# Feed-forward stage of a graph layer: TensorE's output projection ahead of the third chunk of the first layer, and the second layer's first two columns in three chunks

## The chip, the cores and the metric

One Trainium2 chip, one core. The metric is the device time of one execution in microseconds (us), as the median of several runs. An engine executes its own instructions in order; engines wait for each other through semaphores (`wait_ge` on the one side, `then_inc` on the other).

## The reference, cut to what matters

Two graph layers over 12500 nodes of 128 features and 200000 edges. The first is attention over edges and then a feed-forward part; the part that the change touches is:

```python
        att = agg.reshape(n, NH * HD) @ Wo + bo
        x = residual + att
        residual = x
        h = _layer_norm(x, g2, b2)
        ffn = jax.nn.gelu(h @ W1 + bf1, approximate=False) @ W2 + bf2
        return residual + ffn
```

`agg` is the softmax-weighted sum over a node's edges and its own loop. HID is 128, FFN is 512. Around it stand an outer residual and, ahead of the second layer, `relu(layernorm(x))`; its rows go to a table (`h_tab` in the trace, `h2_tab` in the code) that the second layer gathers.

## The kernel before, in words

The kernel goes through its stages in turn: a preparation with queries, keys and values (group_a), the edges of the first layer (batch_b), the nodes of the first layer (group_c), the edges of the second layer (batch_d), the nodes of the second layer (group_e). Each stage has a loop on each engine, and the order of the work on an engine is written out by hand. The change lies in group_c, on TensorE (PE) and on ScalarE (ACT).

group_c goes over 14 groups of 896 nodes; a group is 128 partitions by G = 7 columns of 128 features. Buffers are doubled: group g uses set k = g mod 2. Group g's steps are:

- VectorE (DVE), `attend`: weighs and adds the gathered states, divides, and writes the aggregate `qg` (L1866, counts `agg_s`). It then copies the indices for GpSimd's next gathers (L1868).
- TensorE transposes the seven columns of `qg` (L1335, counts `aggT_ps`), ScalarE copies them (L1154, counts `aggT_s`), TensorE multiplies by `wo` (L1343, counts `att_ps`): this is the projection of attention.
- VectorE, `add_attention`: adds it to the nodes (L1875) and takes their statistics (L238, L243). ScalarE takes the square root (`norm_root`, L248). VectorE inverts it (L254, L256) and writes the normalised rows `hn2` (L1833, counts `hn2_s`).
- TensorE transposes `hn2` (`norm_T`, L1302); ScalarE copies with scale and bias (`norm2_T`, L1113).
- TensorE, `ffn1` (L1311): the first layer in FC = 4 chunks of 128 hidden features, each two matmuls of 448 columns. Chunks alternate between two pairs of PSUM banks, so chunk 2 waits for gelu 0 and chunk 3 for gelu 1. ScalarE, `gelu` (L1143, counts `gelu_s`), one for each chunk.
- TensorE, `ffn2` (L1322): the second layer, seven columns of four chunks each, accumulated in PSUM. It writes the banks that chunks 0 and 2 used. Ahead of column FFN_COLUMNS = 5 it places `norm_T` of the next group.
- VectorE, `add_ffn`: adds the result (L1886) and takes statistics; ScalarE, `norm3` (L1123), writes the normalised rows for the second graph layer, seven columns spread over the gaps between gelus of a later group. SyncE stores them; GpSimd adds the outer residual and the bias by DMA (L904, L910) and gathers the next states (L635).

A 32-bit matmul appears as two instructions in the trace: `ffn1` has 16 rows a group, `ffn2` 56, the projection 14. Transposes have 7.

The groups are interleaved. In turn g, TensorE's order before is: chunks 0 and 1 of group g-1, transposes of group g, chunk 2 of g-1, projection of g, chunk 3 of g-1, five columns of `ffn2` of g-1, `norm_T` of g, two columns of `ffn2` of g-1. ScalarE's order is: `norm2_T` and gelu 0 of g-1, two columns of `norm3`, the copy of the transposes of g, gelus 1 to 3 of g-1 with one column of `norm3` behind each, then the roots (a table load before them), the exponentials of the loops (another table load), an activation that loads the gelu table (a third), and two columns of `norm3`. VectorE's order is `add_attention` of g-1, the scale and `hn2` of g-1, the aggregate of g, `add_ffn` of g-2, and the maxima for g+1.

Of the kernel before, what the change touches and what calls it, by code (L numbers as in the profile page):

```python
# [31 lines left out]
FC = FFN // P  # L32
# [4 lines left out]
G = 7  # L37
# [36 lines left out]
FIRST_COLUMNS = 2  # L74
COLUMNS_BY = (4, 5, 6, G)
FFN_COLUMNS = 5
BANK_COLUMNS = ((0, 4), (4, G))
QKV_BANKS = 4
SHIFT_COLUMN = 3
# [47 lines left out]
def build(nc, a, out):  # L127
    ctx = ExitStack()
    with ctx:
# [79 lines left out]
        def two_banks(b):  # L209

            flat = ps[:, b:b + 2, :].rearrange("p a b -> p (a b)")
            return flat[:, 0:GW], [flat[:, j * HID:(j + 1) * HID] for j in range(G)]
# [7 lines left out]
        def halves(b):  # L220

            return ps[:, b:b + 2, 0:HALF]
# [23 lines left out]
        def norm_root(act, ln, n):  # L246
            act.wait_ge(ln.steps, n * 4 - 2)
            nc.scalar.activation(ln.dev, ln.mean_var[:, :, 1], ACT.Sqrt, bias=eps_t[:]).then_inc(ln.std, 1)  # L248
# [256 lines left out]
        def last_group(g):  # L505
            return isinstance(g, int) and g == 2 * PAIRS - 1
# [461 lines left out]
        def _(act):  # L968
# [141 lines left out]
            def norm2_T(g, k):  # L1110

                act.wait_ge(hnT2_ps, g + 1)
                nc.scalar.activation(xT[k], two_banks(4 * k)[0], ACT.Identity, bias=cols[:, 3:4], scale=cols[:, 2:3])\  # L1113
                    .then_inc(hnT2_s, 1)

            def norm3(g, k, start, stop, stored=None):

                if stored is not None:
                    act.wait_ge(h2_stored[k], stored)
                act.wait_ge(lnC[1].steps, g * 4 + 4)  # L1120
                settle(act)
                for j in range(start, stop):
                    done = nc.scalar.activation(h2b[k][:, j, :], column(nodes, g * G + j), ACT.Relu,  # L1123
                                                bias=nmr3[k][:, j:j + 1], scale=rstd3[k][:, j:j + 1])
                if stop == G:
                    done.then_inc(h2_s, 1)

            def gelus(g, k, norm3_too, start=0, stop=FC):


                for c in range(start, stop):
                    j = COLUMNS_BY[c - 1] if c else FIRST_COLUMNS
                    act.wait_ge(ff1_ps, g * FC + c + 1)
                    gelu(g, k, c)
                    if norm3_too and j < COLUMNS_BY[c]:
                        norm3(g - 2, k, j, COLUMNS_BY[c])

            def loop_exp(g, k):
                act.wait_ge(low1_s, g + 1)
                nc.scalar.activation(w_c[k], low_c[k], ACT.Exp, scale=SCALE).then_inc(w_cs, 1)  # L1140

            def gelu(g, k, c):
                nc.scalar.activation(gT[k][:, c, :].rearrange("p (h f) -> p h f", h=2),  # L1143
                                     halves(4 * k + 2 - 2 * (c % 2)), ACT.Gelu, bias=bf1[:, c:c + 1]).then_inc(gelu_s, 1)

            def group_c(i, first):

                for k in range(2):
                    g = i * 2 + k
                    if not (first and k == 0):  # L1150
                        norm2_T(g - 1, 1 - k)
                        gelus(g - 1, 1 - k, not (isinstance(g, int) and g < 3), 0, 1)
                    act.wait_ge(aggT_ps, g + 1)
                    nc.scalar.copy(xT[k], two_banks(4 * k)[0]).then_inc(aggT_s, 1)  # L1154
                    if not (first and k == 0):
                        gelus(g - 1, 1 - k, not (isinstance(g, int) and g < 3), 1, FC)

                    norm_root(act, lnC[0], g + 1)
                    if not first:
                        norm_root(act, lnC[1], g - 1)  # L1160
                    if not last_group(g):
                        loop_exp(g + 1, 1 - k)
                    nc.scalar.activation(gelu_load, eps_t[:], ACT.Gelu)
                    if not first:
                        norm3(g - 2, k, 0, FIRST_COLUMNS, None if isinstance(i, int) and i == 1 else i * 16 - 16)
            loop_exp(0, 0)
            repeat(act, PAIRS, group_c, peel=2, tail=1)
            norm2_T(2 * PAIRS - 1, 1)
            gelus(2 * PAIRS - 1, 1, True)
# [56 lines left out]
        def _(pe):  # L1226
# [54 lines left out]
            for t in range(2):  # L1281
                done = nc.tensor.matmul(ps[:, t, :], ones[:], diag8[:, 4 * t:4 * t + 4, :].rearrange("p h c -> p (h c)"),  # L1282
                                        start=True, stop=True)
            done.then_inc(chunk_ps, 1)
            pe.wait_ge(chunk_s, 5)
            for h in range(NH):
                done = nc.tensor.transpose(ps[:, 2 + h // 4, (h % 4) * P:(h % 4 + 1) * P], weight[:, h, :], ident[:])
# [3 lines left out]
            for h in range(NH):  # L1291
                nc.tensor.matmul(ps[:, 4, h * HD:(h + 1) * HD], weightT[:, h, :],
                                 stb[LAST][:, B - 1, h * HD:(h + 1) * HD], start=True, stop=True)
                done = nc.tensor.matmul(ps[:, 4, HID + h:HID + h + 1], weightT[:, h, :],
                                        stb[LAST][:, B - 1, HID + h:HID + h + 1], start=True, stop=True)
# [3 lines left out]
            def norm_T(g, k):  # L1299
                pe.wait_ge(hn2_s, g + 1)  # L1300
                for j in range(G):
                    done = nc.tensor.transpose(two_banks(4 * k)[1][j], hn2[:, j, :], ident[:])  # L1302
                done.then_inc(hnT2_ps, 1)

            def ffn1(g, k, chunks):
                pe.wait_ge(hnT2_s, g + 1)
                for c in chunks:
                    if c >= 2:
                        pe.wait_ge(gelu_s, g * FC + c - 1)
                    for h in range(2):  # L1310
                        done = nc.tensor.matmul(halves(4 * k + 2 - 2 * (c % 2))[:, h, :], w1[:, c * P:(c + 1) * P],  # L1311
                                                xT[k][:, h * HALF:(h + 1) * HALF], start=True, stop=True)
                    done.then_inc(ff1_ps, 1)

            def ffn2(g, k, between):

                pe.wait_ge(gelu_s, g * FC + FC)
                for j in range(G):
                    if between and j == FFN_COLUMNS:
                        norm_T(g + 1, 1 - k)  # L1320
                    for c in range(FC):
                        done = nc.tensor.matmul(two_banks(4 * k + 2)[1][j], gT[k][:, c, j * HID:(j + 1) * HID], w2[:, c, :],  # L1322
                                                start=(c == 0), stop=(c == FC - 1))
                done.then_inc(ff2_ps, 1)

            def group_c(i, first):
                for k in range(2):
                    g = i * 2 + k
                    if first and k == 1:
                        norm_T(0, 0)  # L1330
                    if not (first and k == 0):
                        ffn1(g - 1, 1 - k, range(0, 2))
                    pe.wait_ge(agg_s, g + 1)
                    for j in range(G):
                        done = nc.tensor.transpose(two_banks(4 * k)[1][j], qg[k][:, j, :], ident[:])  # L1335
                    done.then_inc(aggT_ps, 1)
                    if not (first and k == 0):
                        ffn1(g - 1, 1 - k, range(2, 3))
                    pe.wait_ge(aggT_s, g + 1)
                    if not first:  # L1340
                        pe.wait_ge(x2_s, g - 1)
                    for j in range(G):
                        done = nc.tensor.matmul(two_banks(4 * k + 2)[1][j], xT[k][:, j * HID:(j + 1) * HID], wo[:],  # L1343
                                                start=True, stop=True)
                    done.then_inc(att_ps, 1)
                    if not (first and k == 0):
                        ffn1(g - 1, 1 - k, range(3, FC))
                        ffn2(g - 1, 1 - k, True)
            repeat(pe, PAIRS, group_c)
            ffn1(2 * PAIRS - 1, 1, range(FC))  # L1350
            ffn2(2 * PAIRS - 1, 1, False)


# [8 lines left out]
            def group_e(i, first):  # L1362
                for k in range(2):
# [12 lines left out]
                    done.then_inc(mlp1_ps, 1)  # L1376
                    for j0, j1 in BANK_COLUMNS:
                        nc.tensor.matmul(flat[:, j0 * HID:j1 * HID].rearrange("p (j f) -> p j f", f=HID), ones[0:1, :],
                                         gb2[0:1, :].unsqueeze(1).to_broadcast([1, j1 - j0, HID]), start=True, stop=False)
                    pe.wait_ge(relu_s, g + 1)  # L1380
                    for j0, j1 in BANK_COLUMNS:
                        for j in range(j0, j1):
# [622 lines left out]
```

## Time and profile before

| | us |
|---|---|
| median of 3 runs | 4827.98 |
| lowest to highest | 4821.74 to 4830.42 |
| the profiled execution | 4826.0 |
| its span in the trace | 4824.4 |

| engine | busy us | share |
|---|---|---|
| PE matmul | 507.4 | 11% |
| PE weight load | 356.6 | 7% |
| DVE | 2847.1 | 59% |
| ACT | 2136.2 | 44% |
| POOL | 3407.3 | 71% |

The shares are means over stages with different limits, so the rows further down are from the stage itself, which lies between about 2400 and 2675 us. A timeline row has its start, how long it lasts, engine, line, operation, the tile written and those read, and the number of instructions merged into it; in brackets stands how long the engine was idle before it and who released it. The end of a row of matmuls lies about 0.15 us past the start of the next, since they are pipelined.

### The profile page before, as it was taken

Reading aid. Unit: us, or ns where it says so; the run is one execution under the profiler, and the core shown is the slowest. Engines: PE = TensorE matmul, PEld = TensorE weight load, DVE = VectorE, ACT = ScalarE, POOL = GpSimd, SP = SyncE. Lnnn points to the kernel's source line nnn. Section 1 sums busy time; section 2 is a strip of 40 time slices with the busy share of each in tenths; the row PEclk is TensorE's granted clock in tenths of the full one; section 3 lists DMA queues with packets and bytes.
Section 4 is the critical chain, followed back from the end, with each engine's and each line's share of the span. In section 5 each row is a group of like instructions: output and inputs, shape, how many; then the busy total and the mean of one; then the engine's idle time right before and its main releaser. Section 6 shows DMA issues by size and latency. Waiting matters only on the chain.

```text
span 4824.4 us, 22224 instructions
## 1 busy us (share of the span) xinstructions
PE 507.4 (11%) x2377; PEld 356.6 (7%) x2377; DVE 2847.1 (59%) x4386; ACT 2136.2 (44%) x2140; POOL 3407.3 (71%) x3610
## 2 busy tenths in 40 slices
PE   4620000000000000000189000000000000000007
PEld 2410000000000000000067000000000000000004
DVE  7837999999999999999778222222222222222223
ACT  4414555454444555554367344444444444444432
POOL 4677777777777777777554677777777777777766
PEclk8655555555555555555599555555555555555558
DMA  9995666666666666666455233333333333333334
GB/s 360 381 370 182 218 211 212 214 214 216 214 213 214 214 214 216 211 211 210 151 119 125 93 102 101 101 105 102 104 104 104 104 104 104 104 104 104 104 98 138
DMA packets 235483, 816.46 MB, mean 169 GB/s; under 512 B 67005, under 2 KB 93789, under 8 KB 185242
## 3 DMA queue, kind: packets, MB, share of 16 engines
q1 hardware_dynamic: 77464, 457.58, 25.5%
q0 software_dynamic: 143232, 344.58, 25.0%
q10 hardware_dynamic: 14722, 13.70, 0.9%
q14 instruction: 57, 0.47, 0.0%
q8 instruction: 8, 0.13, 0.0%
HBM read 455.00 MB, written 354.21 MB: 168 GB/s over the span
## 4 chain that ended last, share of the span: by engine, by line
POOL 42%; issue 19%; DVE 15%; DMA 10%; DVEq 7%; PE 5%; ACT 1%; SPq 0%; POOLq 0%; ACTq 0%
POOL arena L635 41%; DMA q_edges<-arena 7%; DVE ps L1689 4%; DMA arena<-kv_tab,idx 2%; DVE ps L1735 2%; DVE arena L1682 2%; PE ps L1322 2%; PE ps L1311 2%; DVE arena L1751 2%; DVEq L1706 2%; DVEq L1776 2%; DVEq L1718 2%; DVE ps L1631 1%; DVEq L1723 1%; DVE ps L1713 1%
## 5 line engine op out<-in xcount | busy, mean ns | idle before, releaser
L635 POOL DMA_INDIRECT arena<-h_tab,idx x1568 | 1479.7, 944 | 520.4 <-issue 500.1
L635 POOL DMA_INDIRECT arena<-kv_tab,idx x1568 | 1482.6, 946 | 506.9 <-issue 493.5
L1927 DVE SCALAR_TENSOR_TENSOR ps<-arena,keep,ps 128x128 f32<-128x128 f32 x97 | 42.4, 438 | 1486.4 <-ACT ps L1193 1486.4
L1193 ACT COPY ps<-arena 128x2048 f32<-128x2048 f32 x97 | 347.9, 3587 | 768.1 <-DMA arena<-h_tab,idx 768.1
L1206 ACT COPY arena<-arena 128x2048 f32<-128x2048 f32 x97 | 354.2, 3652 | 402.2 <-DVE arena L1934 402.2
L1631 DVE TENSOR_TENSOR_SCAN ps<-arena,ps 128x256 f32<-128x256 f32 (+2 forms) x584 | 502.4, 860 | 0.3
L1058 ACT COPY arena<-arena 128x1024 f32<-128x1024 f32 x196 | 375.4, 1915 | 176.7 <-DVE arena L1751 176.7
L1751 DVE TENSOR_TENSOR_SCAN arena<-arena,ps 128x1024 f32<-128x1024 f32 x196 | 445.5, 2273 | 7.6 <-issue 0.4
L1934 DVE TENSOR_TENSOR_SCAN arena<-arena,ps 128x1024 f32<-128x1024 f32 x194 | 433.0, 2273 | 7.5 <-issue 0.4
L1047 ACT COPY ps<-arena 128x1024 f32<-128x1024 f32 x196 | 363.3, 1886 | 10.1 <-DMA arena<-q_edges 4.0
L1042 ACT COPY arena<-keep 128x960 f32 (+1 forms) x99 | 98.2, 992 | 463.5 <-DVE arena L1751 446.3
L635 POOL DMA_INDIRECT arena<-states,node_idx x196 | 192.2, 980 | 115.1 <-issue 64.1
L1682 DVE TENSOR_TENSOR arena<-arena,ps 128x1024 f32<-128x1024 f32 x196 | 230.5, 1217 | 40.5 <-DMA arena<-kv_tab,idx 35.4
L1735 DVE TENSOR_TENSOR ps<-arena,ps 128x1024 f32<-128x1024 f32 x196 | 239.9, 1224 | 7.3
L1689 DVE TENSOR_REDUCE ps<-arena 128x64 f32<-128x1024 f32 x196 | 230.8, 1223 | 9.4 <-issue 0.5
L1282 PE MATMUL ps<-arena,ones 128*128 128x512 f32 x4 | 3.4, 1018 | 2051.6 <-DVE arena L1656 2051.6
L1357 PE MATMUL ps<-arena 128*128 128x128 f32 x2 | 0.8, 503 | 2002.5 <-ACT arena L1211 2002.5
L635 POOL DMA_INDIRECT arena<-dst_tab,idx x98 | 97.2, 992 | 83.2 <-DVE idx L1554 47.9
L1282 PEld LDWEIGHTS ps<-arena,ones 128*128 128x128 f32 x4 | 1.2, 326 | 2053.0 <-DVE arena L1656 2051.9
L1357 PEld LDWEIGHTS ps<-arena 128*128 128x128 f32 x2 | 0.5, 313 | 2002.8 <-ACT arena L1211 2002.8
L1088 ACT COPY arena<-arena 128x128 f32<-128x128 f32 x98 | 39.9, 407 | 237.6 <-DVE arena L1771 237.6
L639 POOL DMA_INDIRECT q_edges<-arena,start_i x98 | 102.0, 1041 | 54.8 <-issue 30.3
(249 smaller groups left out, 2450.8 us busy)
## 6 DMA issues: line engine op xcount, KB each, us to landing
states<-arena SPq DMA_DIRECT2D x98, 1152.0 KB, 5.4
q_edges<-arena SPq DMA_DIRECT2D x98, 1024.0 KB
arena<-q_edges SPq DMA_DIRECT2D x98, 1024.0 KB, 7.7
states<-arena SPq DMA_DIRECT2D x98, 1024.0 KB, 4.1
arena<-kv_tab,idx POOLq DMA_INDIRECT x1568, 2.8
arena<-h_tab,idx POOLq DMA_INDIRECT x1568, 2.5
kv_tab<-arena ACTq DMA_DIRECT2D x14, 896.0 KB, 9.5
arena<-kv_tab SPq DMA_DIRECT2D x14, 448.0 KB, 5.7
```

The lines of the kernel that those rows point to most:

```text
L635: pool.indirect_dma_start(to, None, tab, bass.IndirectOffsetOnAxis(ap=at, axis=0)).then_inc(done, 16)
L639: pool.indirect_dma_start(tab, bass.IndirectOffsetOnAxis(ap=at, axis=0), frm, None, bounds_check=EP - 1, oob_is_err=False).then_inc(done, 16)
L1047: nc.scalar.copy(q_now[:, fs, :], qb[k][:, :, fs].rearrange("p b f -> p f b")).then_inc(q_turned, 1)
L1058: return nc.scalar.copy(stb[k][:, :, half * HF:(half + 1) * HF].rearrange("p b f -> p f b"), sums_flat[:, half * HF * B:(half + 1) * HF * ...
L1193: nc.scalar.copy(rows_now, rows[k].rearrange("p b f -> p f b")).then_inc(rows_turned, 1)
L1206: done = nc.scalar.copy(sums_b[k].rearrange("p b f -> p f b"), run_sums.rearrange("p (f b) -> p f b", b=B))
L1631: nc.vector.tensor_tensor_scan(part, keep_flat[n % 2][:, 0:(f1 - f0) * B], part, 0.0, ALU.mult, ALU.add)
L1682: done = nc.vector.tensor_tensor(keys, keys, q_now[:, :, b0:b1].rearrange("p f b -> p b f"), ALU.mult)
L1689: nc.vector.tensor_reduce(score[:, :, 1 + b0:1 + b1].rearrange("p h t -> p t h"), kvb[n % 2][:, b0:b1, 0:HID].rearrange("p b (h d) -> p b ...
L1735: done = nc.vector.tensor_tensor(weighed.rearrange("p (h d) b -> p b h d", d=HD), values.rearrange("p b (h d) -> p b h d", d=HD), probs_h[ ...
L1751: done = nc.vector.tensor_tensor_scan(sums_flat[:, half * HF * B:(half + 1) * HF * B], keep_flat[n % 2], weighed_flat, 0.0, ALU.mult, ALU.add)
L1934: done = nc.vector.tensor_tensor_scan(run_sums[:, part], keep1_flat[n % 2], rows_flat[:, part], 0.0, ALU.mult, ALU.add)
```

## The change

On TensorE the transposes of group g come behind chunk 0 of g-1 alone; chunk 1 lies between the transposes and the projection; chunks 2 and 3 follow the projection. `ffn2` goes over its columns in the order 0, 4, 1, 2, 3, 5, 6. For columns 0 and 4, which lie in different banks, it first does chunks 0 to 2 once three gelus are done, then waits for the fourth gelu and does chunk 3. `norm_T` stands ahead of the sixth column of the new order, which is column 5 as before. On ScalarE the two columns of `norm3` that stood ahead of the copy of the transposes stand behind it.

```diff
+EARLY_COLUMNS = 2
+FFN_ORDER = (0, 4, 1, 2, 3, 5, 6)
@@ ScalarE, group_c
                     if not (first and k == 0):
                         norm2_T(g - 1, 1 - k)
-                        gelus(g - 1, 1 - k, not (isinstance(g, int) and g < 3), 0, 1)
+                        gelus(g - 1, 1 - k, False, 0, 1)
                     act.wait_ge(aggT_ps, g + 1)
                     nc.scalar.copy(xT[k], two_banks(4 * k)[0]).then_inc(aggT_s, 1)
                     if not (first and k == 0):
+                        if not (isinstance(g, int) and g < 3):
+                            norm3(g - 3, 1 - k, FIRST_COLUMNS, COLUMNS_BY[0])
                         gelus(g - 1, 1 - k, not (isinstance(g, int) and g < 3), 1, FC)
@@ TensorE, ffn2
-                pe.wait_ge(gelu_s, g * FC + FC)
-                for j in range(G):
-                    if between and j == FFN_COLUMNS:
-                        norm_T(g + 1, 1 - k)
-                    for c in range(FC):
+                def column_part(j, chunks):
+                    for c in chunks:
                         done = nc.tensor.matmul(two_banks(4 * k + 2)[1][j], gT[k][:, c, j * HID:(j + 1) * HID], w2[:, c, :],
                                                 start=(c == 0), stop=(c == FC - 1))
+                    return done
+                pe.wait_ge(gelu_s, g * FC + FC - 1)
+                for j in FFN_ORDER[0:EARLY_COLUMNS]:
+                    column_part(j, range(FC - 1))
+                pe.wait_ge(gelu_s, g * FC + FC)
+                for j in FFN_ORDER[0:EARLY_COLUMNS]:
+                    column_part(j, range(FC - 1, FC))
+                for t, j in list(enumerate(FFN_ORDER))[EARLY_COLUMNS:]:
+                    if between and t == FFN_COLUMNS:
+                        norm_T(g + 1, 1 - k)
+                    done = column_part(j, range(FC))
                 done.then_inc(ff2_ps, 1)
@@ TensorE, group_c
                     if not (first and k == 0):
-                        ffn1(g - 1, 1 - k, range(0, 2))
+                        ffn1(g - 1, 1 - k, range(0, 1))
                     pe.wait_ge(agg_s, g + 1)
                     for j in range(G):
                         done = nc.tensor.transpose(two_banks(4 * k)[1][j], qg[k][:, j, :], ident[:])
                     done.then_inc(aggT_ps, 1)
                     if not (first and k == 0):
-                        ffn1(g - 1, 1 - k, range(2, 3))
+                        ffn1(g - 1, 1 - k, range(1, 2))
                     pe.wait_ge(aggT_s, g + 1)
...
                     done.then_inc(att_ps, 1)
                     if not (first and k == 0):
-                        ffn1(g - 1, 1 - k, range(3, FC))
+                        ffn1(g - 1, 1 - k, range(2, FC))
                         ffn2(g - 1, 1 - k, True)
```

## Rows read from the trace of the kernel before

**Rows 1.** The page, busy tenths of TensorE in 40 slices of the span.
```profile
PE   4620000000000000000189000000000000000007
```
**Rows 2.** Busy time by engine in one turn: PE, PEld, DVE, ACT, POOL; clock, DMA.
```profile
2499.20:2516.10 16.90, 15.80 (x102) 12.24 (x102) 14.29 (x54) 13.23 (x20) 8.68 (x9) 1.00 0.62 139
```
**Rows 3.** Timeline of TensorE through one turn.
```profile
2506.12 1.67 PE L1311 MATMUL ps<-arena,w 128*128 128x448 f32 x4
2508.89 4.73 PE L1322 MATMUL ps<-w,arena 128*128 128x128 f32 x40 [1.10 <-ACT arena L1143]
2513.50 0.98 PE L1302 MATMUL ps<-ident,arena 128*128 128x128 f32 x7
...
2516.11 3.17 PE L1311 MATMUL ps<-arena,w 128*128 128x448 f32 x8
2519.23 0.99 PE L1335 MATMUL ps<-ident,arena 128*128 128x128 f32 x7
2520.05 1.67 PE L1311 MATMUL ps<-arena,w 128*128 128x448 f32 x4
2521.55 1.73 PE L1343 MATMUL ps<-wo,arena 128*128 128x128 f32 x14
2523.11 0.92 PE L1311 MATMUL ps<-arena,w 128*128 128x448 f32 x2
```
**Rows 4.** Timeline of ScalarE in the same turn.
```profile
2507.83 1.01 ACT L1143 ACTIVATE arena<-ps,bf 128x896 f32<-128x896 f32 x1 [1.10 <-PE ps L1311]
...
2509.23 1.28 ACT L248 ACT_TABLE_LOAD   x1
2510.53 0.49 ACT L248 ACTIVATE arena<-arena,eps_t 128x7 f32<-128x7 f32 x2
...
2514.82 1.08 ACT L1113 ACTIVATE arena<-ps,cols 128x896 f32<-128x896 f32 x1
```
**Rows 5.** Timeline of VectorE in the same turn, and two rows of a later one.
```profile
2509.31 0.58 DVE L243 BATCH_NORM_AGGREGATE arena<-arena 128x2 f32<-128x6 f32 x7
2510.97 0.20 DVE L254 RECIPROCAL arena<-arena 128x7 f32<-128x7 f32 x1 [1.08 <-ACT arena L248]
...
2511.55 1.89 DVE L1833 TENSOR_SCALAR arena<-nodes,arena 128x128 f32 x7 [0.18 <-DVE arena L256]
...
2518.08 1.09 DVE L1866 TENSOR_TENSOR arena<-arena 128x896 f32<-128x896 f32 x1
...
2612.55 0.20 DVE L254 RECIPROCAL arena<-arena 128x7 f32<-128x7 f32 x1 [1.23 <-ACT arena L248]
...
2619.45 1.09 DVE L1866 TENSOR_TENSOR arena<-arena 128x896 f32<-128x896 f32 x1
```
**Rows 6.** Timeline, the first turns (ScalarE, VectorE, TensorE) and the last projection's end.
```profile
2440.49 1.01 ACT L1143 ACTIVATE arena<-ps,bf 128x896 f32<-128x896 f32 x1 [1.86 <-PE ps L1311]
...
2443.25 0.20 DVE L254 RECIPROCAL arena<-arena 128x7 f32<-128x7 f32 x1 [0.86 <-ACT arena L248]
...
2449.80 1.09 DVE L1866 TENSOR_TENSOR arena<-arena 128x896 f32<-128x896 f32 x1
...
2455.51 1.67 PE L1311 MATMUL ps<-arena,w 128*128 128x448 f32 x4
...
2641.38 1.67 PE L1311 MATMUL ps<-arena,w 128*128 128x448 f32 x4
```
**Rows 7.** Timeline, the stage's end: the last group's two layers.
```profile
2651.36 6.19 PE L1311 MATMUL ps<-arena,w 128*128 128x448 f32 x16
...
2656.08 1.01 ACT L1143 ACTIVATE arena<-ps,bf 128x896 f32<-128x896 f32 x1
...
2658.66 6.52 PE L1322 MATMUL ps<-w,arena 128*128 128x128 f32 x56 [1.10 <-ACT arena L1143]
```
**Rows 8.** The projection ahead of the loop (timeline), and 20 us of the last stage (windows).
```profile
2416.14 3.36 PE L1343 MATMUL ps<-wo,arena 128*128 128x128 f32 x14 [1.00 <-ACT arena L1154]
...
4720.00:4740.00 20.00, 13.96 (x66) 8.60 (x63) 7.69 (x9) 3.99 (x5) 15.38 (x16) 0.95 0.49 155
```

## The prediction

> **What bounds the kernel now.** I read the page's 40 slices first. TensorE's digits show it at work in three places; only the middle one, slices 21 and 22, is the stage the diff touches [rows 1]. All that the change can move lies there, some 240 of 4824 us. Next I cut the middle stage by period: in one group's 16.9 us TensorE is busy 15.80, VectorE 14.29 and ScalarE 13.23 at a granted clock of 1.00 [rows 2]. TensorE looks like the bound, with 1.10 us idle. The timeline of TensorE shows that this idle time is one gap: before the 40 matmuls of L1322 it waits for the last gelu, L1143 [rows 3]. The change goes for that gap.
>
> A busy share of 93% does not say that nothing else is as late. So I followed the data instead. Attention's projection (L1343) feeds VectorE's L1875 and its statistics; they end in L243; ScalarE takes the root (L248), which waits behind the last gelu; VectorE goes on with L254, normalises (L1833), and forms the next group's aggregate (L1866); TensorE transposes that (L1335) and projects again. Call E the moment at which TensorE starts what follows the projection. One turn, from E = 2506.12 [rows 3]:
> - E to the start of the last gelu: 2507.83 - 2506.12 = 1.71 (the third-column chunk of L1311, x4) [rows 3, 4].
> - last gelu to L254: 2510.97 - 2507.83 = 3.14. In it lie the gelu and one column of L1123 (1.40, until 2509.23), the table load (1.30) and the root with its way to VectorE (0.44) [rows 4, 5]. The statistics were ready at 2509.31 + 0.58 = 2509.89 [rows 5], the root began at 2510.53: **the root is held by ScalarE's own queue**, not by its data.
> - L254 to the end of L1866: 2518.08 + 1.09 - 2510.97 = 8.20 [rows 5]. A later turn has 2619.45 + 1.09 - 2612.55 = 7.99 [rows 5]. I take the middle, 8.10.
> - end of L1866 (2519.17) to the next E (2523.11): 3.94 [rows 3, 5]. This is 0.06 to the start of L1335, then 0.82 for it, 1.50 for a chunk, 1.56 for the projection [rows 3].
> Sum 1.71 + 3.14 + 8.20 + 3.94 = 16.99, which is 2523.11 - 2506.12. So this loop is as long as TensorE's own (15.80 + 1.10 = 16.90) [rows 2, 3]. The two are tied, and the mean period is (2641.38 - 2455.51) / 11 = 16.90 [rows 6].
>
> **The change, part by part.** E(g) is E of group g, 1 to 13; E(2) is 2455.51 and E(13) is 2641.38 [rows 6].
>
> *1. The order of TensorE.* Before: chunk 0, 1, transposes, chunk 2, projection, chunk 3. After: chunk 0, transposes, chunk 1, projection, chunks 2, 3. The number of matmuls is the same. From the end of L1866 to E there are still transposes, one chunk, projection: 3.94, no gain, because the transposes already began 0.06 after L1866. From E to the last gelu there are now two chunks: 1.71 + 1.50 = 3.21. The root stands behind that gelu, so L254 comes at E + 3.21 + 3.14 = E + 6.35, in place of E + 4.85. The statistics' readiness does not matter, it was never last. **New period: 6.35 + 8.10 + 3.94 = 18.39, which is 1.49 more than 16.90**; with 7.99 it is 18.28, with 8.20 it is 18.49 [rows 3 to 5].
>
> *2. The gap before L1322.* It goes: the first twelve matmuls (columns 0 and 4, chunks 0 to 2) need only the third gelu, which starts near E + 1.7 and ends near E + 2.7, before chunk 3 is done at E + 3.0. Twelve take 12 x 4.73/40 = 1.42, to E + 4.4, and the last gelu ends at E + 4.2 (3.21 + 1.01 [rows 4]): no wait at either place. Alone this is worth 1.10 per period, but TensorE is then early for others. The 40 matmuls end at E + 7.6, and L1302 needs L1833, which ends 2.47 after L254 (2511.55 + 1.89 - 2510.97) [rows 5], at E + 8.8: it waits 1.3. After it 2516.11 - 2513.50 = 2.61 for it and the last sixteen [rows 3], E + 11.5; chunk 0 to E + 13.0; then the transposes need L1866 at E + 14.45: 1.5 waited. These two stalls replace one of 1.10. Check: 15.6 to 15.8 of work plus 2.8 is 18.4.
>
> *3. The column order and the two accumulations open at once.* Same matmuls, same weight loads, another bank each turn. No row of before shows two open accumulations; the nearest is the run of 40 at 0.118 each [rows 3], which I take. As the far end I let each of the sixteen early ones cost what a projection's matmul cost at half clock, 3.36/14 = 0.24 [rows 8]: 16 x 0.12 = 2.0 more. The stalls of 1.3 and 1.5 behind them hide even that, so 0 either way; a gain is excluded, since the loop doesn't run through them. Without the stalls it would be 0 to 2.0 per period.
>
> *4. The extra wait on the gelus' count.* Behind it stand the four last-chunk matmuls and the rest of the layer; it costs nothing while the stall at L1302 is 1.3 us. If that cover went, it would cost the few hundredths seen between a gelu's end (2508.84) and L1322's start (2508.89) [rows 3, 4].
>
> *5. ScalarE: two columns of L1123 now come behind the copy of the transposes.* Before, the copy waited for the transposes anyway. After, the transposes end about 1.0 behind L1866, and the copy (0.91) can go at once; the two columns end near 2.8 and push gelu 1 by 0.1 at most, which nothing needs before chunk 3. Cost 0. The copy that starts the next group (L1113) starts 2514.82 - 2507.83 = 6.99 after the last gelu [rows 4], so at E + 10.2, and ends by E + 11.3, just ahead of TensorE's E + 11.5. A narrow margin, but behind it TensorE still waits 1.5 for L1866.
>
> *6. Queues of DMAs.* SyncE's stores and loads and GpSimd's gathers move with the counts that they wait for. GpSimd is busy about 8.7 of 16.9 us [rows 2]; 18.4 gives it more room. 0.
>
> *7. Both ends of the stage.* Start: up to the end of chunk 3 of group 0 TensorE does the same work in another order, so that group's last gelu (2440.49), L254 (2443.25) and L1866 (ends 2450.89) stay [rows 6]. Then E(2) = 2450.89 + 3.94 = 2454.83, against 2455.51. The first two groups have no column of L1123 between gelu and root: last gelu to L254 is 2443.25 - 2440.49 = 2.76 [rows 6], so that E(3) = 2454.83 + 3.21 + 2.76 + 8.10 + 3.94 = 2472.84. Ten periods of 18.39 bring E(13) to 2656.74, against 2641.38: **+15.4**. After E(13) the last group's chunks start at E + 11.5 in place of 2651.36 - 2641.38 = 9.98: **+1.5**. There the early columns help: the 56 matmuls waited from 2657.5 for the gelu until 2658.66; the third gelu ended at 2656.08 + 1.01 = 2657.09 [rows 7]. **-1.15**. What follows the stage (L1886, statistics, root, store, gathers) is one chain and only shifts.
>
> Sum: 15.4 + 1.5 - 1.15 = **+15.7 us** (rounded). The profiled execution took 4826.0 (span 4824.4), so it would be 4841.7; on the median shown, 4827.98, it is 4843.7. Runs of before lie from 4821.7 to 4830.4; I give 4843.
>
> **A rule of the Trainium skill.** A table load and the root begin with nothing between them: 2509.23 + 1.28 = 2510.51, and the root is at 2510.53 [rows 4]. The Trainium skill, ScalarE: Activation LUTs, section What ACT_TABLE_LOAD costs, adds a drain of about 1380 ns to the 1283 ns of each switch of sets. By that rule gelu to L254 would be some 4.5 rather than 3.14; the trace shows no drain on the way in, so the sum keeps 3.14.
>
> **The rivals.**
> *A. The last gelu doesn't hold the root (not slower).* Then TensorE's gap goes and only the statistics bound the root: they are ready at E + 3.77 (2509.89 - 2506.12), L254 follows at E + 4.21, and the period is 4.21 + 8.10 + 3.94 = 16.25, above TensorE's 15.8. That is -0.65 x 11 - 1.15 = -8.3: 4820. For it: 93% busy, and the one idle time of TensorE in a turn is that gap [rows 2, 3]. Against: L1335 starts 0.06 after L1866, and L254 waited 1.08 for the root [rows 3, 5]. It decides if L254 comes before E + 4.86 (16.90 - 8.10 - 3.94), and that needs a root ahead of the last gelu, while ScalarE's order puts it behind. The Trainium skill, TensorE: Matmul & The Clock Gate, section Why this matters for your kernels, asks to keep TensorE busy without breaks, which points the same way as this rival. Chance 6%.
> *B. The loop is longer, but part is taken up (within 0.2%).* Some of the 3.94 or 8.10 shrinks as VectorE's own waits (0.16 each) and the projection's wait go: at most 0.5 per period, or 5 of the 15.7, which leaves 10.7 and 4839; with the runs' scatter against it, 4832. Chance 11%.
> *C. The granted clock falls (much slower).* TensorE would be busy 86% and stall twice. The last stage shows 13.96 of 20 us busy at a clock of 0.95 [rows 8], so more breaks can cost clock. At half clock the projection took 3.36 in place of 1.72 [rows 3, 8]. If transposes, chunk and projection behind the stall (3.9) ran at half clock, each of 11 periods is 3.9 longer: 43 more, 4886. Against: one gap of 1.10 per period leaves 1.00 now. The Trainium skill, TensorE: Matmul & The Clock Gate, section A second HAM failure mode: psum-queue depth-cycling, says that micro-idles between groups of matmuls can make the clock swing. Chance 4%.
> *D. The forecast.* 79%.
>
> **How the numbers follow.** The forecast's own spread: 18.28 to 18.49 gives 1.1 either way, part 3 nothing, the ends of the stage 1, 0.1 in each turn's 3.94 another 1, the scatter of the medians 4 either way: 4836 to 4850. To leave out no more than 2 in 10 the range takes in some of B below and a slight loss of clock above: 4832 to 4854. About 0.2% (9.7 us) is what a measurement can tell from no change. Faster 0.03 (half of A, with scatter); same 0.15 (the rest of A, B and a little of D's low tail); slower 0.82.
>
> **What would show it.** In the profile after: a period of 18.4; L1322 with no wait for L1143 in the middle of the stage; new idle time of about 1.3 before L1302 (released by L1833) and 1.5 before L1335 (by L1866); VectorE's wait before L254 up from 1.08 to about 2.6; granted clock 1.00. It is wrong if the root gets ahead of the last gelu, if L1866 to E is under 3.5, or if the period stays under 17.5.

## The result and the profile after

| | before | after |
|---|---|---|
| median of 7 runs, us | 4826.1 | 4841.81 |
| lowest to highest | 4821.74 to 4830.42 | 4840.05 to 4844.2 |
| profiled execution, us | 4826.0 | 4840.08 |
| its span | 4824.4 | 4838.4 |

The ratio is 1.0032, with a 95% interval of 1.0021 to 1.0044: slower by 15.7 us (10 to 21). The forecast was 15.7 more on the profiled execution, and 4843 in a range of 4832 to 4854. The two profiled executions are 14.1 apart. That the difference of the medians is 15.7 to the digit is luck, since its interval is 11 us wide. The profile says whether the forecast came true for the reasons given.

In the kernel after, the lines are: first layer L1315, second layer L1323, transposes of the aggregate L1347, projection L1355, transposes of the normalised rows L1306, gelu L1145, columns of the later norm L1125, roots L250 and their first reader L256, normalised rows L1845, aggregate L1878.

The timeline of TensorE through one turn, which answers to [rows 3] (start, duration, what, and the idle time with its releaser):

```profile
2507.22 3.17 PE L1315 MATMUL ps<-arena,w 128*128 128x448 f32 x8
2510.23 4.65 PE L1323 MATMUL ps<-w,arena 128*128 128x128 f32 x40
2516.10 0.98 PE L1306 MATMUL ps<-ident,arena 128*128 128x128 f32 x7 [1.22 <-DVE arena L1845]
2516.92 1.95 PE L1323 MATMUL ps<-w,arena 128*128 128x128 f32 x16
2518.70 1.67 PE L1315 MATMUL ps<-arena,w 128*128 128x448 f32 x4
2521.82 0.98 PE L1347 MATMUL ps<-ident,arena 128*128 128x128 f32 x7 [1.45 <-DVE arena L1878]
2522.64 1.67 PE L1315 MATMUL ps<-arena,w 128*128 128x448 f32 x4
2524.15 1.72 PE L1355 MATMUL ps<-wo,arena 128*128 128x128 f32 x14
2525.71 3.17 PE L1315 MATMUL ps<-arena,w 128*128 128x448 f32 x8
```

The 40 matmuls of the second layer follow the chunks without a wait; the gap of 1.10 is gone. In its place stand two, 1.22 ahead of L1306 and 1.45 ahead of L1347, and both are released by VectorE. The turn is 2525.71 - 2507.22 = 18.49.

ScalarE in the same turn, which answers to [rows 4]; the last gelu is the second row:

```profile
2508.92 1.01 ACT L1145 ACTIVATE arena<-ps,bf 128x896 f32<-128x896 f32 x1 [1.61 <-PE ps L1315]
...
2510.43 1.01 ACT L1145 ACTIVATE arena<-ps,bf 128x896 f32<-128x896 f32 x1
2511.33 0.48 ACT L1125 ACTIVATE arena<-nodes,arena 128x128 f32 x1
2511.83 1.28 ACT L250 ACT_TABLE_LOAD   x1
2513.13 0.49 ACT L250 ACTIVATE arena<-arena,eps_t 128x7 f32<-128x7 f32 x2
```

and VectorE, which answers to [rows 5]:

```profile
2510.40 0.58 DVE L245 BATCH_NORM_AGGREGATE arena<-arena 128x2 f32<-128x6 f32 x7
2513.57 0.20 DVE L256 RECIPROCAL arena<-arena 128x7 f32<-128x7 f32 x1 [2.59 <-ACT arena L250]
...
2520.68 1.09 DVE L1878 TENSOR_TENSOR arena<-arena 128x896 f32<-128x896 f32 x1
```

The statistics are ready at 2510.98, the root begins at 2513.13: it waits for the last gelu, a column of L1125 and the table load, and VectorE idles 2.59 where it idled 1.08. The terms of the forecast, read in this turn: E (2507.22) to the last gelu 3.21 (forecast 3.21), gelu to L256 3.14 (3.14), L256 to the end of L1878 (2521.77) 8.20 (7.99 to 8.20), from there to the next E 3.94 (3.94). The windows view of the turn, which answers to [rows 2]:

```profile
2507.22:2525.71 18.49, 15.82 (x102) 12.30 (x101) 14.41 (x53) 13.34 (x21) 8.61 (x10) 1.00 0.57 127
```

The work of TensorE is the same to 0.02 us and the granted clock stays at 1.00; only the turn around it is longer.

The first turns and the last, to hold against [rows 6] and [rows 7]:

```profile
2427.98 3.29 PE L1315 MATMUL ps<-arena,w 128*128 128x448 f32 x4 [1.19 <-ACT arena L1115]
...
2452.49 3.17 PE L1315 MATMUL ps<-arena,w 128*128 128x448 f32 x8
...
2654.32 3.17 PE L1315 MATMUL ps<-arena,w 128*128 128x448 f32 x8
...
2665.81 6.20 PE L1315 MATMUL ps<-arena,w 128*128 128x448 f32 x16
2671.84 6.44 PE L1323 MATMUL ps<-w,arena 128*128 128x128 f32 x56
2678.12 0.27 PE L1366 MATMUL ps<-ident,same_dst 128*128 128x128 f32 x1
```

From the first chunk to the end of the last group's second layer the stage takes 2678.12 - 2427.98 = 250.14 us. Before, the corresponding rows are

```profile
2429.77 5.34 PE L1311 MATMUL ps<-arena,w 128*128 128x448 f32 x8 [1.19 <-ACT arena L1113]
...
2665.01 0.27 PE L1354 MATMUL ps<-ident,same_dst 128*128 128x128 f32 x1
```

or 235.24: +14.9 in the stage, of +14.0 in the span. The stage holds all of it: it began 1.8 earlier in this execution, and what follows it took 0.9 longer.

### The profile page after: what moved, and what is told of

Its sections match the earlier page's. It is cut to its first block, busy times and chain, and to the rows that moved or that the text cites. A ratio compares the mean times of both kernels' runs of the same rounds, so it can differ in the third digit from the quotient of the medians.

```text
span 4838.4 us, 22235 instructions
## 1 busy us (share of the span) xinstructions
PE 498.7 (10%) x2377; PEld 350.7 (7%) x2377; DVE 2846.5 (59%) x4386; ACT 2137.6 (44%) x2140; POOL 3406.3 (70%) x3610
## 4 chain that ended last, share of the span: by engine, by line
POOL 41%; issue 19%; DVE 17%; DMA 10%; DVEq 8%; PE 3%; ACT 1%; SPq 0%; POOLq 0%; ACTq 0%
POOL arena L637 40%; DMA q_edges<-arena 7%; DVE ps L1701 4%; DVE ps L1747 2%; DMA arena<-kv_tab,idx 2%; DVE arena L1763 2%; DVE arena L1694 2%; DVEq L1788 2%; DVEq L1718 2%; DVEq L1730 2%; DVE ps L1643 2%; PE ps L1315 1%; DVEq L1735 1%; DVE ps L1725 1%; DVE arena L1731 1%
```

## The experiments

The question was which part costs the time and through what. Theory T: the order of the chunks alone, because it puts the last gelu, and behind it the root, 1.5 us later in VectorE's loop. The rivals were TensorE's own time, the two open accumulations, and ScalarE's changed order. "Turn" below is the distance from the projection of group 2 to that of group 13, over 11, from each run's timeline of TensorE; it is free of the scatter of the whole program. It is 16.90 before ((2639.82 - 2453.95) / 11) and 18.35 after ((2652.76 - 2450.93) / 11), from these rows, the first two of the kernel before:

```profile
2453.95 1.72 PE L1343 MATMUL ps<-wo,arena 128*128 128x128 f32 x14
...
2639.82 1.72 PE L1343 MATMUL ps<-wo,arena 128*128 128x128 f32 x14
...
2450.93 1.72 PE L1355 MATMUL ps<-wo,arena 128*128 128x128 f32 x14
...
2652.76 1.72 PE L1355 MATMUL ps<-wo,arena 128*128 128x128 f32 x14
```

The ratio is estimated from all executions of both kernels, so it can differ by some ten-thousandths from the quotient of the two medians. Below, "a beside b" gives the median of a run and that of the kernel before, measured together with it.

| run | what it is | ratio to before (95%) | turn, us |
|---|---|---|---|
| after | the change | 1.0032 (1.0021 to 1.0044) | 18.35 |
| e11 | the change again | 1.0039 (1.0025 to 1.0053) | 18.35 |
| e1 | early columns only | 0.9994 (0.9985 to 1.0003) | 16.87 |
| e2 | order of chunks and ScalarE's order, without early columns | 1.0035 (1.0023 to 1.0047) | 18.35 |
| e3 | ScalarE's order only | 0.9995 (0.9986 to 1.0004) | 16.90 |
| e4 | e1, and a column off the root's way | 0.9984 (0.9975 to 0.9993) | 16.53 |
| e12 | e4 again | 0.9992 (0.9983 to 1.0001) | 16.54 |
| e5 | after, and a column off the root's way | 1.0025 (1.0016 to 1.0034) | 18.00 |
| e6 | after, no root | 0.9979 (0.9970 to 0.9988) | 16.25 |
| e7 | before, no root | 0.9997 (0.9988 to 1.0006) | 16.73 |
| e8 | e1, no root | 0.9966 (0.9954 to 0.9978) | 15.92 |
| e9 | e6 without the bias's DMA | 0.9970 (0.9959 to 0.9981) | 15.90 |
| e10 | e8 without the bias's DMA | 0.9974 (0.9964 to 0.9984) | 15.92 |

### The three parts, one at a time: e1, e2, e3

e1 against the kernel before takes the second layer's part alone (the whole diff of `ffn2` in the change, nothing else; this is the part that counts):

```diff
+                pe.wait_ge(gelu_s, g * FC + FC - 1)
+                for j in FFN_ORDER[0:EARLY_COLUMNS]:
+                    column_part(j, range(FC - 1))
                 pe.wait_ge(gelu_s, g * FC + FC)
...
```

> The kernel before with only the second layer's part of the change: columns 0 and 4 in three chunks ahead of the last gelu, TensorE's chunks of the first layer and ScalarE's order as before. Theory T (the root stands behind the last gelu, and the order of the chunks moves that gelu by 1.5 us): the gap of 1.10 before L1322 goes, but the loop over VectorE stays at 1.71 + 3.14 + 8.10 + 3.94 = 16.89 per turn against 16.90, so only the end of the stage gains, 1.2 to 1.4: 1 to 3 us faster than before. Rival TensorE (TensorE's busy time alone bounds a turn): 1.10 x 12, 13 us faster. Rival accumulations (the two open accumulations cost the 15.7 us): 10 to 16 us slower than before.

Measured: 4829.45 beside 4832.26. Its waits in the middle of the stage (who waited for whom, us in all, times, longest):

```profile
DVE arena L256 <- ACT arena L250: 11.3, 10, 1.2
PE ps L1304 <- DVE arena L1843: 11.0, 9, 1.3
```

The gap ahead of the second layer is gone, and a gap of 1.22 stands ahead of the transposes of the normalised rows (L1304) instead. The turn is 16.87: what TensorE gained it waits for a few us later. The rival TensorE, 13 us faster, and the rival accumulations, 10 slower, both fall, since the interval goes from 7 us faster to 1 slower. Of the 1 to 3 us expected the whole time shows nothing clear of its scatter. In the trace the last group takes 12.31 (2651.63 to 2663.94) where it took 13.65 before; that is the gain at the end of the stage.

e2 takes the order and leaves `ffn2` as it was. It is the kernel after without the change in `ffn2`, so ScalarE's two lines (e3, below) are in it too; against the kernel before its part on TensorE is:

```diff
-                        ffn1(g - 1, 1 - k, range(0, 2))
+                        ffn1(g - 1, 1 - k, range(0, 1))
...
-                        ffn1(g - 1, 1 - k, range(2, 3))
+                        ffn1(g - 1, 1 - k, range(1, 2))
...
-                        ffn1(g - 1, 1 - k, range(3, FC))
+                        ffn1(g - 1, 1 - k, range(2, FC))
```

> The kernel after with the second layer as it was before: all columns wait for the last gelu. Theory T: turns stay at 18.4, since the stall at L1302 shrinks by what the gap before L1322 takes (the 40 then end at E + 8.9, and the normalised rows come at E + 8.8); at the stage's end the gain of 1.35 is lost: 16 to 18 us slower than before, about 1.3 slower than after. Rival TensorE: the gap is back, no time gained or lost against before by the order itself, within 3 us of before. Rival accumulations: the cost goes, within 3 us of before.

Measured: 4851.61 beside 4832.26. The order, with ScalarE's lines, costs the whole price. TensorE in this kernel:

```profile
2528.70 0.98 PE L1339 MATMUL ps<-ident,arena 128*128 128x128 f32 x7 [1.45 <-DVE arena L1870]
...
2532.59 3.17 PE L1315 MATMUL ps<-arena,w 128*128 128x448 f32 x8
2536.86 4.73 PE L1326 MATMUL ps<-w,arena 128*128 128x128 f32 x40 [1.10 <-ACT arena L1145]
2541.47 0.98 PE L1306 MATMUL ps<-ident,arena 128*128 128x128 f32 x7
```

Here the gap of 1.10 is back and the one ahead of L1306 is away; the wait for VectorE ahead of the transposes of the aggregate (L1339 here) stays, 1.45 in the first row. It is the same 18.35 per turn with the idle time in another place. The 1.3 us expected from the stage's end are not resolved in the whole times (1.0035 and 1.0032), but they stand in the trace: the last group takes 13.65 here (2672.68 to 2686.33) and 12.31 in the kernel after.

e3 takes only ScalarE's two lines:

```diff
-                        gelus(g - 1, 1 - k, not (isinstance(g, int) and g < 3), 0, 1)
+                        gelus(g - 1, 1 - k, False, 0, 1)
...
+                        if not (isinstance(g, int) and g < 3):
+                            norm3(g - 3, 1 - k, FIRST_COLUMNS, COLUMNS_BY[0])
```

> The kernel before with only ScalarE's part: the two columns of L1123 behind the copy of the transposes. Theory T: gelu 1 starts 0.8 later and the others less, the last still starts when its chunk is done: within 2 us of before. Rival ScalarE (this part is what costs): 5 to 16 us slower than before.

Measured: 4829.97 beside 4832.26, turn 16.90. It costs nothing that these runs can tell. The order of the chunks without ScalarE's lines was not run; that these lines cost nothing in the new order either is read from the trace of after, where the last gelu starts at 2510.43, at the end of its chunk (2507.22 + 3.17 = 2510.39).

### Less work between the last gelu and the root: e4, e5

If the root's place in ScalarE's queue sets the turn, any instruction taken out from ahead of it must shorten the turn, in either order of the chunks. The column of L1123 behind the last gelu moves to the next turn, into ScalarE's wait for a chunk (the call with `late` true for the last three chunks, and the column of the last turn, are left out here):

```diff
-                    if norm3_too and j < COLUMNS_BY[c]:
+                    if norm3_too and j < COLUMNS_BY[c] and not (late and c == FC - 1):
...
                         norm2_T(g - 1, 1 - k)
+                        if not (isinstance(g, int) and g < 4):
+                            norm3(g - 4, k, COLUMNS_BY[FC - 2], G)
...
```

> e1 with one thing more: the column of L1123 that stands between the last gelu and the table load of the roots goes to the next turn, behind L1113, where ScalarE waits for a chunk. Theory T: 0.48 to 0.50 less between the last gelu and the root in each of ten turns, 16.4 per turn: 6 us faster than before, 5 faster than e1. Rival TensorE: no change against e1, because ScalarE's place doesn't matter.

> e4 once more. Its turn was 16.53, so theory T gives 5 to 6 us faster than before; if the first measurement was scatter, 0 to 2 us.

> The kernel after, with the column of L1123 between the last gelu and the roots' table load moved to the next turn behind L1113. Theory T: 0.49 less per turn in ten turns: 17.9 per turn, 5 us faster than after, 11 slower than before. Rivals in which the cost lies on TensorE (open accumulations, breaks between matmuls): as after, 15 to 16 slower than before.

Measured: e4 4827.16 beside 4832.26, e12 4819.77 beside 4824.08, e5 4838.86 beside 4825.36. The turns fall by 0.34 (16.87 to 16.53) and 0.35 (18.35 to 18.00). ScalarE in e5:

```profile
2530.97 1.01 ACT L1145 ACTIVATE arena<-ps,bf 128x896 f32<-128x896 f32 x1
2532.00 1.28 ACT L250 ACT_TABLE_LOAD   x1
2533.30 0.49 ACT L250 ACTIVATE arena<-arena,eps_t 128x7 f32<-128x7 f32 x2
```

From the gelu's start to the table load it is now 1.03 where it was 1.40 (2510.43 to 2511.83): 0.37, not the 0.48 to 0.50 expected. The column had begun 0.90 after the gelu's start, while the gelu was still running; the table load begins only behind the gelu's end. Ten turns of 0.37 are 3.7 us, or 0.34 a turn on eleven: this is what the turns show. The direction and the place are as T has them; the dose was set too high by a third. In whole times e5 and after are not separated (1.0025 and 1.0032); there the verdict rests on the turns. e4's gain is separated from before in the first measurement (3 to 12 us by its interval) and at its edge in the second, where 4 us were found and 5 to 6 expected.

### No root at all: e6, e7, e8

These leave the square root of both norms and its table load out and take the reciprocal of the variance on VectorE, so the output is wrong in scale. The way over ScalarE is cut. The diff is shortened to the branch that these runs take; the waits for an old gelu or an old store, which stand in for the root where buffers are overwritten, are left out:

```diff
-            dve.wait_ge(ln.std, n)
+            dve.wait_ge(ln.steps, n * 4 - 2)
             settle(dve)
-            nc.vector.reciprocal(rstd, ln.dev).then_inc(ln.steps, 1)
+            nc.vector.reciprocal(rstd, ln.mean_var[:, :, 1]).then_inc(ln.steps, 1)
```

> The kernel after without the square root in both norms of the stage: VectorE takes the reciprocal of the variance itself, so the values are wrong in scale, and ScalarE's root and its table load are left out; VectorE waits for an old gelu in place of the root where it overwrites buffers. Theory T: VectorE goes on at E + 3.9 whatever the order of the chunks; a turn is 3.9 + 8.1 + 3.94 = 15.9 to 16.0, near TensorE's 15.8: 12 us faster than the kernel before, 27 faster than after. Rivals on TensorE: at most the small change of VectorE's chain, still 10 to 16 slower than before.

> The kernel before without the square root in both norms of the stage, as in e6 (the values are wrong in scale). Theory T: the loop over VectorE is 15.9, but TensorE's 15.8 + 1.10 of waiting for the last gelu stays: 16.9 per turn, so within 3 us of before (the end of the stage loses two roots from its chain, 0.5 each). If the loops weren't tied, and VectorE's loop alone bound the turn, it would be 10 us faster.

> e1 (order of before, early columns) without the square root, as in e6 (the values are wrong in scale). Theory T: both bounds are away, 15.9 to 16.0 per turn: 12 us faster than before, and equal to e6 within 2 us, since without the root the order of the chunks costs nothing. If the order costs something by itself, e6 is slower than e8 by that.

Measured: e6 4815.66, e7 4824.73, e8 4809.75, beside 4825.36. With the root cut, the kernel after falls from 1.0032 to 0.9979, the kernel before stays where it was (TensorE still has its 1.10 gap), and the early columns alone reach 0.9966. So the order costs its 15 us only on a way that leads through the root. That it is the root's place in the queue, and not ScalarE's work as such, rests on e4 and e5; a kernel with the root ahead of the last gelu was not tried. The waits of e7 in the middle of the stage:

```profile
PE ps L1323 <- ACT arena L1148: 11.0, 10, 1.1
DVE nodes L1878 <- PE ps L1344: 10.3, 10, 1.5
```

VectorE now waits for the projection, and TensorE for the last gelu: the other of the two tied loops, alone. It takes 16.73; VectorE's loop, alone in e1, takes 16.87.

One thing didn't fit: e6 and e8 were expected within 2 us of each other, at 12 faster than before, but e6 gained 10 us and e8 16, and e6's turn is 16.25, e8's 15.92. The waits of e6:

```profile
PE ps L1348 <- DVE arena L1881: 6.4, 9, 1.3
DVE nodes L1901 <- DMA nodes<-arena: 4.4, 6, 1.3
```

VectorE waits ahead of L1901 for the DMA that adds the bias to the nodes.

### The DMA behind it: e9, e10, with the change again, e11

```diff
-                pool.dma_start(nodes[:, bass.ds(g * G, G), :], bias_rows, accum_op=ALU.add).then_inc(bias_added[k], 16)
+                pool.sem_inc(bias_added[k], 16)
```

> e6 with the DMA that adds the second layer's bias to the nodes left out as well (its count is given at once; the values are wrong by the bias and in scale). In e6 VectorE waited before L1901 for that DMA, 4.4 us in six turns of nine, and its turn was 16.25 against 15.92 in e8. Theory DMA: that wait is what sets e6 behind e8, so the turn comes to 15.9, 3 to 4 us faster than e6. Rival: the order of the chunks costs 0.3 by itself even without the root; then the turn stays near 16.2.

> e8 with the same DMA left out. Both theories: e8 has no such wait, so its turn stays at 15.8 to 15.9 and the time within 2 us of e8; under theory DMA e9 and e10 are equal within 2 us.

> The kernel after once more, beside the others on one chip: 14 to 17 us slower than before, turn 18.35.

Measured: e9 4810.85, e10 4812.19, e11 4844.8, beside 4824.08. The rows of e9 and then of e10 from which the turn is taken:

```profile
2452.06 1.72 PE L1356 MATMUL ps<-wo,arena 128*128 128x128 f32 x14
...
2626.94 1.72 PE L1356 MATMUL ps<-wo,arena 128*128 128x128 f32 x14
...
2454.93 1.72 PE L1354 MATMUL ps<-wo,arena 128*128 128x128 f32 x14
...
2630.00 1.72 PE L1354 MATMUL ps<-wo,arena 128*128 128x128 f32 x14
```

Without that DMA the two orders have the same turn, 15.90 and 15.92: with neither the root nor the DMA in the way the order of the chunks costs nothing per turn. The whole times of e9 and e10 lie within 1.4 us of each other, and e10's is 0.0008 above e8's with intervals that overlap, so it says only that nothing large changed. e11 has the turn of the kernel after, 18.35, but its median is 20.7 slower than before where 14 to 17 were expected; its interval, 12 to 26 us, takes in the 15.7, and its stage is in part longer by a start that the next section comes to.

## Why the prediction was right

It was right in the result and in its reasons.

- **What bounds the kernel.** Two tied loops, not TensorE's busy share. e1 opens one of them and gains nothing per turn; e7 opens the other and gains 0.17 per turn; e8 opens both and gains 0.98. This is the proof of the tie. It is not quite even: alone, TensorE's loop takes 16.73 (e7), VectorE's 16.87 (e1), and the forecast had 16.90 for TensorE's, since it took a turn in which TensorE already waited a little for VectorE: both runs of transposes take 0.98 to 0.99 in it [rows 3], and 0.93 in e7 and in the first turns of the kernel before, which last 16.73.
- **Part 1, the turn.** 18.39 forecast. From group 3 to 13 it is (2654.32 - 2470.37) / 10 = 18.40, with E(3) = 2470.37 from the timeline. e2 shows that the order has this price without the early columns, and e3 that ScalarE's lines have none by themselves.
- **Part 2, the gaps.** 1.3 and 1.5 forecast, 1.22 and 1.45 found, with the releasers named.
- **Parts 3 to 6.** All at nothing: e1 for the open accumulations and the extra wait (the run of 40 takes 4.65, before 4.73), e3 for ScalarE's order. GpSimd's gathers and DMAs cost nothing in this change, as forecast: no wait of VectorE for a DMA stands in the middle of the stage. e6 and e9 show that with the order of after the bias's DMA is the next thing to hold VectorE once the root is gone; in e8, with the order of before, it doesn't, although the turn is shorter.
- **Part 7, the start.** From the first chunk (2427.98) to E(2) (2452.49) it is 24.51, before 2455.51 - 2429.77 = 25.74: -1.23, where -0.68 was forecast. The term itself is there: from the last gelu of group 0 to E(2) it is 14.34 (2452.49 - 2438.15), before 15.02 (2455.51 - 2440.49), -0.68. The other 0.55 lies ahead of that gelu, where the forecast had nothing: 10.17 from the first chunk, before 10.72. There TensorE's clock rises from 1.2 to 2.4 GHz, and not always at the same matmul. In the kernel after, only the first chunk ran at the lower clock (3.29; 1.67 for the second, with a granted clock of 1.00 from 2431.10 to 2433.38). In e11, the same kernel, the transposes did too (0.50 from 2433.40 to 2434.86), and part of the second chunk (2.24, at a mean of 0.72); there first chunk to gelu takes 11.48, and gelu to E(2) 14.35. So the 0.55 is scatter. e4 and e12, one kernel too, differ by 1.42 in the way to E(2) (26.39 and 24.97).
- **Part 7, the rest.** From E(2) to E(13) it is 201.83 against 185.87, +15.96, and 201.82 in e11; the forecast had 201.91. E(13) to the last group's chunks: 11.49 against 9.98, +1.51 as forecast. The last group: 2678.12 - 2665.81 = 12.31 against 2665.01 - 2651.36 = 13.65, -1.34 where -1.15 was forecast. Together -1.23 + 15.96 + 1.51 - 1.34 = 14.9; with e11 for after it would be 251.44 - 235.24 = 16.2.
- **The rule on the table load.** The Trainium skill, ScalarE: Activation LUTs, section What ACT_TABLE_LOAD costs, adds a drain of about 1380 ns to each switch. Here again the load begins at 2511.83, takes 1.28, and the root starts at 2513.13. The measurement decides: 1.3 is the price between gelu's column and root. A part of such a drain may lie ahead of the load, since it waits for the gelu's end, but in e5 that is 0.13 (1.03 less 0.90).
- **The rivals.** A (the last gelu doesn't hold the root) fell with e1 and e2. Its arithmetic for a turn in which only the statistics bound the root, 16.25, happens to be e6's turn, but by another cause: e8 and e9 have 15.9. The estimate took the root's hop of 0.44 along, which e6 to e10 leave out. B (part of the 15.7 is taken up) fell with the turn: in the turn shown, 3.94 and 8.20 are what they were, and the mean turn is 18.40. C (the clock) fell too: 1.00 with two gaps per turn.

For part 7, the first and the second chunk of the stage in e11, to hold against the first row of the kernel after:

```profile
2430.23 3.35 PE L1315 MATMUL ps<-arena,w 128*128 128x448 f32 x4 [1.19 <-ACT arena L1115]
...
2434.86 2.24 PE L1315 MATMUL ps<-arena,w 128*128 128x448 f32 x4
```

Where the expectations of the runs were wrong is the dose in e4 and e5, 0.37 instead of 0.49. The column's whole place in the queue, 0.50 (2511.33 to 2511.83), was taken as the gain, but without it the table load has to wait for the gelu's end, which is 0.13 later than the column could start.

## What to carry to other kernels

Before an idle gap of the busiest engine is filled, follow one item of data around the whole loop and add it up; if that loop is as long as the turn, the gap will only move, as it did in e1 (1.10 ahead of the second layer, then 1.22 ahead of the transposes). Moving work behind a step on one engine also moves whatever another in-order engine has queued behind the result of that work: here two small roots stood behind a gelu that had nothing to do with them, and 1.5 us of matmuls ahead of that gelu cost 1.5 us in each turn. Where an engine's queue holds a short step of a long loop, take the work ahead of it away as well as opening the other loop. e4 does both and was 0.8 to 1.6 parts in 1000 faster than the kernel before; the first step alone was not run.

## What the runs showed of the hardware

- An ACTIVATE of 128x896 takes 1.01 us, but the next one starts 0.90 after its start, while a table load waits for its end: a small ACTIVATE between the two cost 0.37 us although it lasts 0.48.
- A DMA of 448 KB that adds to memory in SBUF landed 6.9 us (median) after its issue in e6 and 6.0 in e8. In e6 VectorE waited for it in six turns of nine, in e8, with a shorter turn, in none. That it sets e6 back is shown by e9; why it lands later in e6 is open.
- TensorE's granted clock stayed at full level, 1.00, with 15.82 us busy in 18.49 and idle gaps of 1.22 and 1.45.
- Two executions of one program got the full clock at different matmuls at the stage's start, directly behind the first chunk in after and within the second in e11, and from the first chunk to E(2) it took 1.3 us longer in e11.
